# Identity products on TensorE in gaps of a four-layer Flamingo block

## The reference, cut to what matters

```
x = x + tanh(g_xattn[l]) * attention_l(layernorm(x), ctx)
x = x + tanh(g_ffn[l])   * ffn_l(layernorm(x))
```

## Time and profile before

| what | us |
|---|---|
| median of 3 runs | 1488.6 (1488.59 to 1489.28) |
| profiled execution | 1493.37 |
| its span | 1491.7 |
| TensorE busy | 1341.2 (90%) |
| VectorE busy | 1028.4 (69%) |
| ScalarE busy | 797.6 (53%) |
| GpSimd busy | 668.4 (45%) |
| share of the chain of waits in TensorE | 59% |

### The profile page before, as it was taken

The page is one execution under the profiler, slowest core; times in us unless marked ns, Lnnn a source line. Parts: engine busy times, 40 slices in busy tenths (PEclk is TensorE's granted clock), DMA queues, the critical chain, the costliest instruction groups (busy, mean ns, idle before and its releaser), DMA issues.

```text
span 1491.7 us, 23008 instructions
## 1 busy us (share of the span) xinstructions
PE 1341.2 (90%) x7114; PEld 1097.1 (74%) x7114; DVE 1028.4 (69%) x2191; ACT 797.6 (53%) x1980; POOL 668.4 (45%) x675
## 2 busy tenths in 40 slices
PE   5987999998899999977899889999989899999884
PEld 3545888786487878756788567888877788888774
DVE  7786556455687777757645667878888777876644
ACT  6744222222566666653222466767767777786332
POOL 1010554543343434325632145566557767665343
PEclk9997999998999999997999999999999999999797
DMA  6222555562200000010111199000120001023283
GB/s 215 92 92 57 178 159 164 155 183 60 78 8 22 8 15 1 2 43 15 43 43 28 53 284 253 2 1 16 42 79 29 29 29 58 29 96 122 72 271 116
DMA packets 66705, 120.80 MB, mean 81 GB/s; under 512 B 6644, under 2 KB 35976, under 8 KB 65579
## 3 DMA queue, kind: packets, MB, share of 16 engines
q1 hardware_dynamic: 64347, 115.33, 24.9%
q0 software_dynamic: 2256, 4.22, 0.8%
HBM read 82.53 MB, written 38.96 MB: 81 GB/s over the span
## 4 chain that ended last, share of the span: by engine, by line
PE 59%; DVE 17%; issue 7%; DMA 6%; ACT 5%; POOL 4%; SPq 1%; POOLq 0%; DVEq 0%; ACTq 0%
PE ps L1469 8%; PE ps L1442 8%; PE ps L1420 7%; PE ps L1487 6%; PE ps L1341 5%; PE ps L1285 5%; PE ps L1452 4%; DMA w<-in_l1f_w 4%; PE ps L1147 3%; PE ps L1431 3%; PE ps L1301 2%; PE ps L1355 2%; POOL urs L905 2%; PE ps L1665 2%; DVE usum L2834 1%
## 5 line engine op out<-in xcount | busy, mean ns | idle before, releaser
L912 POOL TENSOR_TENSOR probs<-probs,prec 128x512 f32<-128x512 f32 x192 | 201.9, 1052 | 323.7 <-DVE prec L2866 323.5
L2056 ACT ACTIVATE probs<-ps,nmax 128x256 f32<-128x256 f32 x384 | 178.6, 471 | 217.8 <-DVE nmax L2859 217.5
L1469 PE MATMUL ps<-probs_t,v_tok 128*128 128x256 f32 x768 | 200.7, 385 | 0.2 <-ACT ob L2075 0.2
L1442 PE MATMUL ps<-k_feat,q_feat 128*128 128x256 f32 x768 | 198.6, 381 | 1.9 <-ACT q_feat L2047 1.9
L905 POOL TENSOR_TENSOR urs<-uve,neg_half 128x4 f32<-128x4 f32 x136 | 136.9, 1007 | 56.4 <-DVE uve L2835 45.7
L2859 DVE TENSOR_REDUCE nmax<-ps 128x2 f32<-128x512 f32 x192 | 131.6, 686 | 31.1 <-PE ps L1442 28.2
L1442 PEld LDWEIGHTS ps<-k_feat,q_feat 128*128 128x128 f32 x768 | 137.4, 191 | 16.0 <-issue 2.7
L1452 PEld LDWEIGHTS ps<-ident,probs 128*128 128x128 f32 x768 | 93.8, 142 | 64.9 <-issue 36.6
L1469 PEld LDWEIGHTS ps<-probs_t,v_tok 128*128 128x128 f32 x768 | 132.9, 193 | 10.9 <-ACT probs_t L2065 0.4
L1452 PE MATMUL ps<-ident,probs 128*128 128x128 f32 x768 | 117.7, 276 | 20.9 <-ACT probs_t L2065 20.5
L2065 ACT ACTIVATE probs_t<-ps 128x512 f32<-128x512 f32 x192 | 115.1, 600 | 3.1 <-PE ps L1452 3.1
(11 more groups left out here) (399 smaller groups left out, 3637.3 us busy)
## 6 DMA issues: line engine op xcount, KB each, us to landing
rows_in<-zero_rows SPq DMA_DIRECT2D x3, 5160.0 KB, 42.1
tile_w<-in_l3f_w SPq DMA_DIRECT2D x21, 385.5 KB, 7.0
w<-in_l1f_w SPq DMA_DIRECT2D x24, 256.0 KB, 6.4
spread_w<-we_dram SPq DMA_DIRECT2D x16, 384.0 KB, 3.8
kv_cross<-kv_out SPq DMA_DIRECT2D x20, 256.0 KB, 2.0
kv_first<-kv_out SPq DMA_DIRECT2D x16, 256.0 KB, 2.0
spread_w<-we_dram SPq DMA_DIRECT2D x16, 256.0 KB, 4.2
w<-in_l2f_w SPq DMA_DIRECT2D x8, 512.0 KB, 3.5
```

The source lines that it names most:

```text
L912: pool.tensor_tensor(p3, p3, spread(prec[g % 3][:, :], [P, TB, S]), ALU.mult)\
L1442: mm = pe.matmul(ps[g % 2][:, j * S:(j + 1) * S], q_feat[:, h, j * P:(j + 1) * P], k_feat[:, kv, :], start=True, stop=True)
L1469: mm = pe.matmul(ps[6][:, 0:S], v_tok[:, tb, kv * P:(kv + 1) * P], probs_t[g % 2][:, tb, :], start=tb == 0, stop=tb == TB - 1)
L2056: ins = act_e.activation(probs[g % 4][:, j, :], ps[g % 2][:, j * S:(j + 1) * S], ACT.Exp, bias=nmax[g % 3][:, j:j + 1], accum_out=psums[g ...
```

## The change

A new function in TensorE's program multiplies the identity by the identity, `count` times, into the first 128 columns of a bank that holds nothing needed then; nobody reads the result, and the calls wait for nothing. It is called in twelve places: in the layer 1 attention (18 before the turn of the last part, 4 behind the turn of the third and of the last part), before `turn_fourth(0)` (4), in `fourth(b)` before the turn of part b+1 (14 for b = 0, then 4 and 4), before the first `turn_unit` of the first attention (32), before its last `turn_probs` (14), before the turn of the second mixture (32), before `feat_ready` (9) and before its experts (54). That is 193 products. Nothing else is changed.

```
--- before.py
+++ after.py
@@ -1075,6 +1075,11 @@
             jobs = [0]
             pe.wait_ge(const_ready, 4)
 
+            def keep_clock(count, bank):
+
+                for _ in range(count):
+                    pe.matmul(ps[bank][:, 0:P], ident[:, :], ident[:, :], start=True, stop=True)
+
             def turn_half(tok, half, ready, value):
 
                 pe.wait_ge(ready, value)
@@ -1186,6 +1191,7 @@
             def fourth(b):
 
                 if b < B - 1:
+                    keep_clock(14 if b == 0 else 4, 5)
                     turn_fourth(b + 1)
                 pe.wait_ge(part_out, 3 * B + b + 1)
                 for i in range(TB):
@@ -1246,11 +1252,16 @@
             pe.matmul(ps[5][:, S:S + 1], ones_row[:, :], tot_max[:, :], start=True, stop=True).then_inc(max_out, 1)
             early(1)
             for b in range(B):
+                if b == B - 1:
+                    keep_clock(18, 5)
                 turn_part(2, b, z[:, :].rearrange("p (t d) -> p t d", d=D), whole_rounded, b + 1)
                 if b < 2:
                     early(1)
+                else:
+                    keep_clock(4, 5)
                 pe.wait_ge(c_whole, b // 2 + 1)
                 product(2, b, q_whole, lambda kb: cq_whole[:, b * TB + kb, :])
+            keep_clock(4, 5)
             turn_fourth(0)
             for b in range(B):
                 fourth(b)
@@ -1424,6 +1435,8 @@
 
                 def turn_unit(u):
                     r = f.unit(u)[4]
+                    if f.biased and r == 0:
+                        keep_clock(32, 4)
                     pe.wait_ge(s["norm_ready"], r + 1)
                     if r:
                         pe.wait_ge(s["turn_out"], r)
@@ -1444,6 +1457,8 @@
                     mm.then_inc(s["s_ready"], 1)
 
                 def turn_probs(g):
+                    if f.biased and g == f.total - 1:
+                        keep_clock(14, 5)
                     pe.wait_ge(s["p_ready"], g + 1)
                     if g:
                         pe.wait_ge(s["pt_out"], g)
@@ -1530,9 +1545,12 @@
 
             packed_experts(L1F)
             run(attention(L2X, begin_late(FIRST_LN, h_tok)))
+            keep_clock(32, 6)
             turn(h_tok, h_ready, (1, 2))
+            keep_clock(9, 6)
             feat_ready()
             logits(wg2, 8)
+            keep_clock(54, 6)
             experts(L2F)
             def last_gates(i):
```

## The result

The changed kernel takes 1491.64 us (median of 20 runs, 1485.82 to 1500.18), the kernel before 1486.59 on the same chip (20 runs, 1481.85 to 1498.36). The ratio is 1.0035, 95% interval 1.002 to 1.005: slower by 5.2 us, between 3.0 and 7.4. The direction was as forecast; the forecast of +8.4 us was too high. The changed kernel's profiled execution took 1497.44 us.

What follows compares the result with a forecast made beforehand. TensorE was busy for 90% of the span, mostly at full clock; only low-clock time on the chain counts. 0.0 + 0.4 + 3.1 + 2.4 + 2.5 = +8.4 us on the median 1488.6 gave 1497.0; own range 1492.6 to 1500.6, stretched 1488.5 to 1501.5.

Steps and rivals of the forecast that it cites:

- half price: Rival, all fills: a call costs 0.11 us as one MATMUL, so -3.1 us in all, 1485.5; chance 0.08.
- The products do not hold the clock: Rival, all fills: calls cost 0.43 us and the clock is not held, 1543 us; chance 0.03.
- The clock falls inside A: Rival, first mixture: TensorE idles between turns, so the clock falls all the same, +3.5 more, 1500.5; chance 0.10.
- A: First mixture's opening: gain -1.5, slow products after a new idle +1.5, together 0.0; bounds -1.5 and +2.0 (two such spells).
- C: First attention's end: 14 calls where TensorE has no gap, all on the chain, +3.1 us, up to +4.5.
- D: Second mixture, before the tokens' turn: 32 calls, 7.2 us, in an idle of 4.41; +2.4 us.
- delay absorbed: Rival: VectorE and GpSimd hide E, a wait for loads part of C and D; +2 us, 1490.6; chance 0.12.
- B: First attention's opening: 32 calls make the turn 2.7 us late, full clock gains 2.3; +0.4 us.
- E: Before the second mixture's experts: 54 calls, clock falls, first two units end after the third is due; +2.5 us, bounds 0 and +3.5.
- With 4.6: 11 calls until 681.6, 43 more by 691.3: Step of E: clock back 4.6 us after 677.0, 11 calls slow until then, 43 more ending by 691.3.

Runs made afterwards that it cites:

- e6: The changed kernel without its five fills of 4 calls: 1500.79 us, one execution.
- e1: The changed kernel without the 14 calls before the last turn of probabilities: 1489.81 us, ratio 1.0034 to the kernel before.
- after: The changed kernel's own first profile, with all 193 calls: profiled execution 1497.44 us.
- e8: The kernel before, unchanged, profiled a second time: 1483.86 us, one execution.
- e10: The kernel before, unchanged, profiled a third time: 1485.61 us, one execution.
- e2: The changed kernel with 20 calls instead of 32 in the attention's opening and 19 instead of 32 before the second mixture's turn: 1487.35 us, ratio 0.9992.
- e4: The changed kernel with 13 calls more, in the new idle before the expert weights are turned: 1489.2 us, ratio 1.0021 to the kernel before.
- e9: The changed kernel itself, timed and profiled once more: 1491.24 us, ratio 1.0038 to the kernel before.
- e5: The changed kernel with fills cut to their gaps, the 14 replaced by 9 a head earlier, new idle filled, 9 and 54 left out: 1482.11 us, ratio 0.9941.
- e11: e5 with 40 calls put back before the second mixture's experts: 1479.71 us, ratio 0.995 to the kernel before.
- e7: The changed kernel with twice as many turns of the identity in place of its products: 1494.09 us, one execution.

## Why the prediction was right, and where it was not

**Direction and mechanism: right.** A call is two MATMULs and costs 0.223 us at full clock (0.225 was taken). The Trainium skill's 81 ns (TensorE: Matmul & The Clock Gate, Back-to-back issue gap), by which the prediction estimated a sum of about +2 without showing its terms, is not what these f32 products show: 112 ns. Rival "half price" is out: 386 MATMULs from 193 calls. "The products do not hold the clock" is out: 17 us at 1.00 from 115.0. "The clock falls inside A" is out for the changed kernel, and e6 shows that it would have been true without the fills of 4.

**C, +3.1: measured +3.12**, and e1 takes exactly that back. **D, +2.4: measured +2.16** in the profile of after (2.2 to 2.3 against e8 and e10), and e2 takes 2.5 back. Nothing behind the two covered the delay, as argued; "delay absorbed" is out for these two. **B, +0.4: +0.18**, or +0.75 against e8 and e10, whose B was shorter because the clock fell later there, behind the first turns (0.66 us instead of 1.11). The prediction took one execution's low stretch for the kernel's.

**E, +2.5: +0.53. This is the term that was mis-sized.** The step that failed was "With 4.6: 11 calls until 681.6, 43 more by 691.3", that is, where the low stretch begins (1.9 us into the small products) and how long it lasts behind them. In the changed kernel the small products start at 672.18, but the clock falls at 675.5, when they are almost over (1.9 us would have been 674.1), and it is back by 678.9, 2.8 us after the calls began at 676.08; taken were 4.6 us from 677.0. Only some 17 MATMULs of both kinds were slow, the calls ended at 689.47, and the third unit started at 695.03. In e1 and e2 the clock was down for twice as long in the same instructions, and there E is +2.1: almost my term. Of the seven profiles with these 54 calls and products or turns in them, five show 0.2 to 0.5 and two 2.1. I took one length of a low stretch from one execution where the chip shows two. The two long ones began 3.0 (e1) and 2.4 us (e2) after the first small product, the five short ones 3.3 to 4.2. Whether chance or the edits of e1 and e2 ahead of this place made them begin sooner stays open.

**A, 0.0: +1.15 in one profile, -0.04 in the other.** The gain that was put at -1.5 is 1.7 (e4, the same fills with the new idle covered); the prediction's own steps, 0.05 early and 1.66 less for the sixteen products, add up to 1.7 too. The new idle was forecast at 3.1 us and is 3.15. The stretch it causes was put at 1.5 and measured 2.9 and 1.7 (A in the changed kernel and in e9, less A in e4). Again it is the length of the low stretch, 6.7 or 3.2 us, that differs. The upper bound had room for that, with two such spells.

**The sum.** By place it was 7.2 us in the first pair of profiles. With e9 against the mean of the three befores it is A 0, B +0.6, C +3.1, D +2.2, E +0.5, 6.4 in all. So 2 of the 8.4 are E's. What is left between 6.4 and the measured 5.2 lies inside the interval of 3.0 to 7.4; the stages that no edit touched scatter by more than that, and whether they hold a small gain of the change stays open.

**The absolute number.** The measured 1491.64 lies under the forecast's own range of 1492.6 to 1500.6, and inside the second one, 1488.5 to 1501.5, which was stretched to take in a rival. (The bounds of the five terms add up to +4.4 and +12.8, not +4 and +12.) 1497.0 was made on a profiled execution carried to a median of three runs, 1488.6. Over 20 runs the kernel before has 1486.59, and its executions go from 1481.85 to 1498.36, while the three that I had lay within 0.7 us. So 2 us of the miss are from there and 3 from the sum.

**Why the change loses.** It gives back clock where VectorE or ScalarE sets the pace (second mixture), puts 3.1 us where TensorE has no gap (C), overfills two gaps of 4.5 us with 7.2 (B, D), and where it does win (A) overfills too, by 1.5 us, and opens an idle that takes the gain. e5 and e11 keep the idea and mend these: by their ratios 8.8 us faster than the kernel before (4.5 to 13.1) in e5, 7.4 (4.5 to 10.4) in e11.

## What to carry to other kernels

Filling a wait of TensorE with products pays only up to the length of the wait: count the calls from the measured idle, so that they end a few tenths before the releaser (0.17 to 0.26 us here), and look which wait comes next once the stage is faster. A fill is worth what the products behind it gain on the chain, so first find out whether TensorE or another engine ends the stage. Judge such an edit by stages between fixed instructions in several profiles, since the whole scatters by more than 10 us between executions, and one fill is worth 0.5 to 3 us.

## What the runs showed of the hardware that was not expected

A stretch at the lower clock comes in two lengths here for the same instructions, about 3.3 and 6.7 us (after and e9 before the weights' turn; after and e1 at the second mixture's small products). That alone moves a stage by 1.2 to 1.6 us between executions. Nor does it begin at a fixed instruction: after the same idle of 4.48 us it took in the first turns of B in one profile of the kernel before and began behind them in the two others, and after the same 2.15 us at C it came in ten profiles and not in the eleventh (e6). The second mixture's small products did not bring the clock back by themselves: in e11 they run at 0.50 throughout, 7.0 us, after an idle of 2.22, and in the changed kernel the clock fell while they ran, after an idle of 0.79. Turns of the identity hold the clock, and bring it back, as its products do (e7). And the loop of the first mixture takes 210 to 220 us in different executions of code that is the same; no run here was made to find out why.
